# A state-space layer and a routed low-rank projection on one core: the order of two peeled steps, the place of one operand split, and the bank borders are changed

## The reference, cut to what matters

```
# layer 0: for each head a kernel k (sum of 64 damped modes), causal convolution of the masked rows
u  = x * (sample < length[seq]);  y = causal_conv(u, k[head]) + u * D[head]
x  = x + y * mask
# layer 1: a dense projection, and two of eight low-rank experts, picked per row
logits = x @ Wr.T + 5.0 * onehot(language);  gates = softmax over the top 2
x  = x + x @ W.T + 2.0 * sum_e gates[e] * (x @ A[e].T) @ B[e].T
```

## Time and profile before

| what | value |
|---|---|
| time, median of 3 runs | 715.37 us (712.67 to 715.88) |
| the profiled execution: its time | 714.37 us |
| the profiled execution: its span, first to last instruction | 712.6 us |
| busy share of the span: PE, DVE, ACT, POOL | 91%, 70%, 65%, 3% |
| mean granted clock of TensorE | 0.975 of full |

### The profile page before, as it was taken

How to read it: one execution, slowest core, us unless ns; L and a number is a source line. 1 busy time by engine, 2 the same in 40 slices (tenths; PEclk the granted TensorE clock), 3 DMA queues, 4 the chain that set the end, 5 groups by cost and what they waited for, 6 DMA issues and landing times.

```text
span 712.6 us, 12371 instructions
## 1 busy us (share of the span) xinstructions
PE 648.1 (91%) x3629; PEld 617.4 (87%) x3629; DVE 495.3 (70%) x1518; ACT 464.9 (65%) x980; POOL 19.1 (3%) x38
## 2 busy tenths in 40 slices
PE   3679778999999999999999999999999999999997
PEld 2478668899898989999898989989898989989997
DVE  8885665776776777766777768676777777676641
ACT  5875666767576767757577766757677776754431
POOL 0000000000000000000000000000000000000000
PEclk9699988999999999999999999999999999999999
DMA  6521122111223222123222221122232211222112
GB/s 184 165 60 31 37 67 68 33 54 47 66 66 66 66 66 41 46 45 66 66 66 66 66 52 47 34 66 66 66 66 66 61 29 57 52 66 38 39 29 60
DMA packets 23904, 43.40 MB, mean 61 GB/s; under 512 B 9896, under 2 KB 14544, under 8 KB 23888
## 3 DMA queue, kind: packets, MB, share of 16 engines
q1 hardware_dynamic: 18608, 26.42, 16.1%
q10 hardware_dynamic: 5280, 16.78, 9.5%
HBM read 26.35 MB, written 16.85 MB: 61 GB/s over the span
## 4 chain that ended last, share of the span: by engine, by line
DVE 34%; PE 22%; issue 21%; ACT 21%; DVEq 1%; ACTq 1%; DMA 0%; SPq 0%
PE pc L1159 13%; DVE state L885 11%; ACT swapped L479 9%; PE pmg L1220 7%; DVE xt L926 5%; ACT s_hi L501 3%; DVE u_lo L837 3%; ACT state L487 3%; ACT L668 2%; DVE t_lo L842 2%; DVE zo_lo L848 2%; DVE gate L959 1%; DVE held L918 1%; DVE k_col L857 1%; DVE c_lo L858 1%
## 5 line engine op out<-in xcount | busy, mean ns | idle before, releaser
L1220 PE MATMUL pmg<-w_hi,y_hi 128*128 128x388 f32 (+1 forms) x768 | 267.4, 348 | 3.1 <-DVE w_lo L828 3.1
L1220 PE MATMUL pmg<-w_lo,y_hi 128*128 128x388 f32 (+1 forms) x768 | 261.7, 341 | 0.0
L1220 PE MATMUL pmg<-w_hi,y_lo 128*128 128x388 f32 (+1 forms) x768 | 261.6, 341 | 0.0
L1220 PEld LDWEIGHTS pmg<-w_hi,y_hi 128*128 128x128 f32 x768 | 145.9, 190 | 4.1 <-DVE w_lo L828 3.6
L1220 PEld LDWEIGHTS pmg<-w_hi,y_lo 128*128 128x128 f32 x768 | 145.9, 190 | 0.4
L1220 PEld LDWEIGHTS pmg<-w_lo,y_hi 128*128 128x128 f32 x768 | 145.6, 190 | 0.0
L479 ACT ACTIVATE swapped<-state 64x128 f32<-64x128 f32 x192 | 59.3, 309 | 87.3 <-DVE state L885 86.0
L524 ACT ACTIVATE result<-pmg 128x388 f32<-128x388 f32 (+1 forms) x96 | 43.2, 452 | 71.8 <-PE pmg L1207 71.3
L885 DVE SCALAR_TENSOR_TENSOR state<-swapped,scan_tab,state 128x192 f32<-128x192 f32 (+1 forms) x240 | 73.8, 349 | 17.1 <-ACT swapped L479 12.7
L918 DVE COPY held<-lang_f 128x1 f32<-128x1 f32 x96 | 14.8, 154 | 78.5 <-PE pc L1159 76.3
L914 DVE TENSOR_TENSOR s_lo<-state,s_hi 128x896 fp32r<-128x896 f32 x32 | 35.0, 1092 | 35.5 <-ACT s_hi L501 35.5
(11 more groups left out here) (206 smaller groups left out, 1068.6 us busy)
## 6 DMA issues: line engine op xcount, KB each, us to landing
rows<-in_x SPq DMA_DIRECT2D x64, 256.0 KB, 5.4
out<-result ACTq DMA_DIRECT2D x62, 256.0 KB, 3.8
toe<-kpad SPq DMA_DIRECT2D x30, 128.0 KB, 5.2
rows<-in_L_cond_W SPq DMA_DIRECT2D x3, 512.0 KB, 6.5
result<-in_L_cond_W SPq DMA_DIRECT2D x3, 512.0 KB, 6.0
w_rows<-in_L_cond_W SPq DMA_DIRECT2D x2, 512.0 KB, 4.4
result<-in_L_cond_A SPq DMA_DIRECT2D x1, 512.0 KB, 5.7
b_rows<-in_L_cond_B SPq DMA_DIRECT2D x2, 256.0 KB, 6.7
```

What stands on the lines that cost most here:

```text
L1220: ins = nc.tensor.matmul(pm[:, n, 0:o1 - o0], y[s][:, c, :], w[:, c, o0:o1], start=(c == 0 and y is y_hi and w is w_hi), stop=(c == CH - 1 ...
```

## The change

- **Banks.** The 1160 columns of the weights (1024 outputs, 128 for A, 8 for the router) are cut at 384 and 768 instead of 388 and 776, so the banks are 384, 384 and 392 wide instead of 388, 388 and 384. Bank 0 then needs the weight tiles 0 to 2 only.
- **Head of a step.** In the loop and behind it `split_toe(b, m + 1)` stands first in a step on ACT and DVE; before, it stood behind `ratios` on ACT and behind `route` and `split_rows` on DVE.
- **The peeled steps** get new orders on ACT, DVE, PE and SP. The powers of the third group of heads are made straight from the table `tab` with no staged copy, and its steps are pulled forward; the output of pair 0 is stored from SP's queue instead of ACT's.
- **GpSimd.** The conversion of the lengths, the mask `valid` (eight instructions of 128x64), `bias` and the sorting of B (eight copies of 128x128) move to POOL from DVE and ACT. Names `vec` in that block are POOL's.

```diff
-BANKS = [(0, 388), (388, 776), (776, WCOLS)]
+BANKS = [(0, 384), (384, 768), (768, WCOLS)]
...
@@ SP
             load_toe(0, 2)
+            sp.wait_ge(px_full, 3)
+            load_rows(0, 4)
+            sp.wait_ge(pm_free, 6)
+            for h in range(2):
+                sp.dma_start(bass.AP(out.tensor, h * LEN, [[HEADS * LEN, SEQS], [1, LEN]]),
+                             result[0][h * SEQS:(h + 1) * SEQS, :]).then_inc(result_dma[0], 16)
+            store_kernel(0, 3)
+            load_toe(0, 3)
...
@@ POOL
+            pool.wait_ge(small_in, 48)
+            pool.wait_ge(consts, 4)
+            vec.tensor_copy(len_f[:, :], len_i[:, :]).then_inc(masks, 1)
+            vec.tensor_copy(lang_f[:, :], lang_i[:, :]).then_inc(masks, 1)
+            pool.wait_ge(masks, 2)
+            for c in range(CH):
+                ins = vec.tensor_scalar(valid[:, c, :], len_f[:, :], sample_no[:, c:c + 1], 0.0, ALU.subtract, ALU.max)
+            ins.then_inc(masks, 1)
+            vec.tensor_scalar(bias[:, :], expert_no[:, :], lang_f[:, :], LANG_BIAS, ALU.is_equal, ALU.mult
+                              ).then_inc(masks, 1)
+            pool.wait_ge(b_in, 32)
+            for o in range(8):
+                vec.tensor_copy(b_sorted[:, o, :, :], b_rows[:, :, o, :]).then_inc(b_ready, 1)
...
@@ ACT, peeled
             turn_first_powers(1)
+            copy_states(0, 0, first=True)
             weight(1)
-            copy_states(0, 0, first=True)
...
-            sort_b()
+            turns_of(1, False, range(2, 4))
...
+            waves(1)
             split_y(0, 0)
             weight(4)
+            weight(5)
+            split_toe(0, 1, toe_rows_back)
             copy_states(0, 1)
-            weight(5)
+            weight(6)
             swap_odd(0, 1, 0)
-            turns_of(1, False)
-            weight(6)
+            magnitudes(1, False, reused=True)
...
+            turns_of(2, False)
+            split_rows(0, 2)
+            split_y(0, 1)
+            split_ctr(0, 2)
+            split_obs(0, 2)
             evacuate(0, 0, 0)
             evacuate(0, 0, 1)
-            split_y(0, 1)
-            split_rows(0, 2)
-            split_ctr(0, 2)
-            split_obs(0, 2)
...
@@ ACT, in the loop and behind it; DVE's has the same line at its head, and loses the one behind split_rows
             def step(b, m, rows_left=True, kernels=True):
+                split_toe(b, m + 1)
                 if rows_left:
                     split_ctr(b, m + 2)
...
                 ratios(b, m)
-                split_toe(b, m + 1)
...
@@ DVE, peeled
             rotate_first_powers(1)
-            low_weight(1)
-            split_ctr(0, 1, kernel=False)
             dve.wait_ge(chunk_ready, 1)
             scanning = scan_states(0, 0, staged=False)
             next(scanning)
+            split_ctr(0, 1, kernel=False)
+            low_weight(1)
...
             low_weight(10)
+            rotate_powers(1, False)
             split_gated(0, 0)
             merge(0, 1)
-            rotate_powers(1, False)
+            angles(2)
+            split_rows(0, 2)
             split_y(0, 1)
-            split_rows(0, 2)
             split_ctr(0, 2)
...
@@ PE, peeled
             turn_weight(4)
-            control(0, 1)
             pe.wait_ge(merged, 1)
             turn_weight(5)
+            control(0, 1)
...
-            pe.wait_ge(wlo_ready, w_tile(3) + 1)
+            pe.wait_ge(wlo_ready, w_tile(2) + 1)
             project(0, 0, 1, 0, 4)
...
             pe.wait_ge(wlo_ready, WTILES)
+            turn_rows(0, 2)
             project(0, 0, 2, 0, 4)
-            turn_rows(0, 2)
+            pe.wait_ge(gthi_ready, 1)
+            pe.wait_ge(gtlo_ready, 1)
+            turn_powers(0, 2)
...
-            turn_powers(0, 2)
             control(0, 2)
...
-            project(0, 1, 0, 0, 4)
+            project(0, 1, 0)
             turn_rows(0, 3)
-            project(0, 1, 0, 4, 8)
             project(0, 1, 1)
+            project(0, 1, 2, 0, 4)
             turn_gates(0, 1, 4)
             convolve(0, 2)
             add_loras(0, 1)
             control(0, 3)
-            project(0, 1, 2, 0, 7)
+            project(0, 1, 2, 4, 8)
```

More of the change, by code:

```diff
@@ L340, in step @@
                 load_toe(b, m + 3)
-            with sp.Fori(0, LOOPS) as b:
+            step(0, 1)
+            with sp.Fori(1, LOOPS) as b:
                 for m in range(2):
@@ L369, in stage_scan @@
                                 ).then_inc(scan_staged, 1)
-            with pool.Fori(0, LOOPS) as b:
+            pool.wait_ge(scan, SCAN * 2)
+            stage_scan(1)
+            with pool.Fori(1, LOOPS) as b:
                 pool.wait_ge(z2_ready, b + 2)
@@ L592, in _ @@
             swap_odd(0, 1, 2)
-            waves(1)
             weight(8)
-            split_toe(0, 1, toe_rows_back)
             split_states(0, 1)
             weight(9)
-            magnitudes(1, False, reused=True)
+            swap_powers(1)
             ratios(0, 0)
             weight(10)
+            turn_powers(1, False)
             split_gated(0, 0)
-            swap_powers(1)
-            turn_powers(1, False)
+            turns_of(2, False)
[3 more added lines that the diff above has]
+            split_obs(0, 2)
             evacuate(0, 0, 0)
             evacuate(0, 0, 1)
-            split_y(0, 1)
-            split_rows(0, 2)
-            split_ctr(0, 2)
-            split_obs(0, 2)
[L610 to L615, removed]
+            magnitudes(2, False, reused=True)
             split_obs(0, 3)
             evacuate(0, 0, 2)
-            split_rows(0, 3)
[L619 to L624, removed]
+            copy_states(0, 2)
+            split_ctr(0, 3)
+            waves(2)
+            swap_odd(0, 2, 0)
+            swap_odd(0, 2, 1)
+            nc.scalar.activation(warm[:, :], phase[:, 0:1], ACT.Exp)
+            swap_odd(0, 2, 2)
+            split_states(0, 2)
+            split_toe(0, 2)
+            swap_powers(2)
+            ratios(0, 1)
+            split_rows(0, 3)
             split_gated(0, 1)
-            waves(2)
+            turn_powers(2, False)
             evacuate(0, 1, 0)
@@ L630, in _ @@
             copy_states(0, 3)
[L631 to L636, removed]
+            for n in range(3):
+                swap_odd(0, 3, n)
             split_states(0, 3)
             def step(b, m, rows_left=True, kernels=True):
+                split_toe(b, m + 1)
                 if rows_left:
@@ L1019, in _ @@
             low_weight(4)
+            low_weight(5)
+            split_toe(0, 1, toe_rows_back)
             scanning = scan_states(0, 1, staged=False)
             next(scanning)
-            low_weight(5)
+            low_weight(6)
             next(scanning)
-            low_weight(6)
-            angles(1)
+            powers(1)
             next(scanning)
@@ L1043, in _ @@
             dve.wait_ge(scan_staged, 1)
-            for _ in scan_states(0, 2):
-                pass
+            scanning = scan_states(0, 2)
+            next(scanning)
+            split_obs(0, 3)
+            split_ctr(0, 3)
+            next(scanning)
+            powers(2)
+            next(scanning)
+            next(scanning)
             split_states(0, 2)
-            split_ctr(0, 3)
-            split_obs(0, 3)
+            split_toe(0, 2)
             route(0, 1)
             split_rows(0, 3)
-            split_toe(0, 2)
-            angles(2)
             split_gated(0, 1)
+            rotate_powers(2, False)
             merge(0, 2)
-            powers(2)
             split_y(0, 2)
@@ L1102, in turn_weight @@
                                   B_: (b_ready, b_sorted)}[what]
-                pe.wait_ge(loaded, 1 if what == B_ else 16)
+                pe.wait_ge(loaded, 8 if what == B_ else 16)
                 before = [j for j in range(k) if TILE[j][1] is place]
@@ L1278, in _ @@
             turn_weight(7)
+            project(0, 0, 0, 6, 8)
             pe.wait_ge(v_copied, 2)
```

36 lines of the change are left out of this document (10 added, 26 removed).

## The result

The changed kernel takes 671.31 us (median of 4 runs, 671.07 to 673.04); the kernel before takes 714.71 in the same call (712.67 to 715.88). The ratio is 0.9401, with a 95% interval of 0.9373 to 0.9429. The profiled execution took 673.04 us, with a span of 671.2 us at a granted clock of 0.983; the one before had 714.37, 712.6 and 0.975. Profiled against profiled, 41.3 us are gone. The changed kernel's own runs, here and in e5, lie at two values, about 673.1 at a clock of 0.983 and about 671.1 at 0.989 to 0.993.

A forecast was written before the change was run, and what follows sets the result against it. PE was taken to bound the kernel, with 23 us of t_lo waits in the loop and 17 us idle in the peeled steps. 714.4 - 24.1 - 19.7 = 670.6, so 671 us; forecast 665 to 675 (chance 0.62), ends 664 and 688.

The forecast's parts named there:

- The split at the head: In the loop, t_lo is held by DVE's order alone; moving it to the step's head saves 24.1 us.
- Shorter step: Loop step occurring 14 times: the gap of 0.74 us before the convolution shrinks, saving 0.7 us each (0.6 to 0.71).
- Longer step: Second step of each loop iteration, 13 times: saves 1.1 us each (0.95 to 1.2), a 0.3 us wait for gated staying.
- the wait moves rather than goes: Loop: t_lo ahead of route makes gated late in both kinds of step; 12 us saved, 683 us; chance 0.08.
- Bank borders: Bank widths cost nothing in the loop; in the peel, bank 0 loses its 2.25 us wait for W's fourth block.
- The peeled steps: First convolution to pair 3's: new orders bring pair 3's convolution to 100.5 from 120.2 us, 19.7 us saved.
- the floor and its waits: Peeled steps: full-clock work 62.1 us plus half clock and waits gives 69.7, from 31.9; pair 3's convolution at 101.6.
- placement: Peeled steps: operations placed with their traced durations, without queue latencies, put pair 3's convolution at 99.4 us.
- The rival with only half of the peel's gain: Peeled steps: a missed wait holds PE, most likely w_lo tiles between scan rounds; 10 us gained, 680 us; chance 0.17.
- The rival of a late sort: GpSimd sorts B late, delaying turn_weight(9); slower from 94 us on, 718 us if ending at 98; chance 0.03.
- DVE pays nothing: Head of the kernel: POOL waits for DVE and DVE's own times stay unchanged, so nothing was taken on DVE.
- The rival that hung on it: Head: DVE and POOL hold each other up, so scans of pairs 0 and 1 come later; +4 us, 675; chance 0.08.

The follow-up runs named there:

- e5: The changed kernel run again without any edit; 673.12 us, ratio 0.9414 to the kernel before.
- e1: The kernel before with one edit, the Toeplitz split at the head of a step in the loop and behind it; 692.98 us, ratio 0.97.
- e2: The changed kernel with the Toeplitz split put back behind route and ratios in the loop; 696.75 us, ratio 0.9744 to the kernel before.
- e3: The changed kernel with bank borders back at 388 and 776 and the wait for the fourth block of W; 673.83 us.
- e8: The changed kernel with the loop's powers behind route on DVE and ACT's Exp table load behind copy_states; 664.36 us, ratio 0.9306 to the kernel before.
- e7: The changed kernel with ACT's Exp table load in the loop moved earlier, right behind copy_states; 666.45 us, ratio 0.9337 to the kernel before.
- e9: The changed kernel with DVE's t_lo between route and u_lo, ACT's half of the split staying at the head; 670.05 us.
- e6: The changed kernel with the powers of the next chunk behind route in DVE's loop; 666.27 us, ratio 0.9322 to the kernel before.
- e11: The changed kernel with powers behind route and the Exp table load earlier, in the loop and also in the peeled steps; 664.8 us.
- e4: The changed kernel with GpSimd's work back: masks on DVE, B sorted by one ACT instruction between two swaps; 674.87 us.
- e10: The changed kernel with only the sorting of B back on ACT, the masks staying on GpSimd; 675.99 us.

## Why the prediction was right, step by step

**The sum.** Forecast from the profiled execution: 24.1 off in the loop, 19.7 in the peel, 43.8 in all. Measured between the two spans: behind the convolution of pair 3, 712.6 - 120.23 = 592.4 became 671.2 - 101.84 = 569.4, 23.0 less; ahead of it 18.4 less. That is 41.4, and 41.3 in the time. The forecast of 671 met the median of 671.31, but not for every reason. The profiled executions would have said 670.6 and measured 673.04, and 1.3 of the difference is in the peel, 1.1 in the loop.

**The split at the head.** Right in mechanism and nearly in size. e1 alone gives 23.0, and in e2 the waits come back. Shorter step: 19.83 to 19.13 is 0.70, forecast 0.7. Longer step: 20.71 to 19.70 is 1.01, forecast 1.1 with bounds of 0.95 to 1.2. The forecast for two steps was 38.8 and 38.83 was measured. The term that was too big is the longer step's. I had `gated` and the transpose moved by 0.34 us and the convolution 0.14 us behind the transpose. A wait of 0.18 us is left (forecast 0.3), and the convolution starts 0.24 us behind it: those 0.1 us, 13 times, are the 1.1 us by which 24.1 was too much. The rival "the wait moves rather than goes" is out: it needed 39.6 us for two steps.

**Bank borders.** Costed at nothing in the loop, and at nothing they came (e3: 19.68 and 19.12). Their use in the peel, the wait at 51.85 of the earlier trace rows, is there: 2.51 us come back without them.

**The peeled steps.** Two estimates stood side by side, and I took 100.5 between 101.6 (the floor and its waits) and 99.4 (placement). Measured was 101.84. The sum of floor and waits seems right, but its terms missed and cancelled:

| term of the peeled steps, us | forecast | changed kernel |
|---|---|---|
| PE's waits | 5.9 | 4.5 |
| lost at half clock | 1.7 | 4.5 (estimate) |
| PE's work at full clock | 62.1 | 61.0 (estimate) |
| from the first convolution to pair 3's | 69.7 | 69.96 |

The second row is worked out from the stretches shown above: 2 x (0.12 x 24.10 + 0.08 x 20.34) = 9.0 us at the half level, and half of it lost; the third is what is left. So the term that was mis-sized is the clock, by 2.8 us. Of the single waits, 0.5, 0.3 and 0.4 were forecast and 0.44, 0.35 and 0.39 measured; 2.1 for `gated` at pair 2 measured 2.00; 1.5 at pair 3 measured 0.92. The 1.1 for `merge` is not listed in the changed kernel (0.41 in e5, 0.73 in e8), and 0.29 for pair 3's state at 90.81 was not forecast. The first convolution was forecast at 31.9 and came at 31.88; nine executions of the same code up to there lie between 31.69 and 32.16, so the last digits are luck. The rival with only half of the peel's gain would have put pair 3 near 110; it is out.

**What I missed there is the clock.** I wrote that it would be at full from some 37 us on. In the profiled execution it was 0.92 from 81.5 to 101.84, and 0.50 from 82 to 84 us: behind the wait of 2.00 us, the matmuls of pair 2's convolution ran at the half level of 1.2 GHz. This is the tile's summary for the convolution of pair 2 in the changed kernel (times in ns: min, median, max):

```profile
L1171 PE MATMUL pc<-u_hi,t_lo x2: 572/600/628, 81.9 to 83.2; 128*128 128x512 f32 x2
```

The same instructions in e8, in which this part of the program is the same:

```profile
L1171 PE MATMUL pc<-u_hi,t_lo x2: 393/396/398, 82.1 to 82.8; 128*128 128x512 f32 x2
```

In e7, e8 and e9 the step from pair 2 to pair 3 takes 18.87 to 19.02 us, in the changed kernel, e5 and e6 20.44 to 20.47, with the same peeled code and the same wait (1.95 to 2.01 us). So the fall of the clock costs 1.5 us, and it comes or not by the execution; what decides it is open. Without it pair 3's convolution comes at 99.79, 100.44 and 100.39: the forecast of 100.5 is met where the clock stays up, as I had assumed, and missed by the clock's 1.5 us where it falls. It can be part of the 2 us between a run of 671.1 at 0.99 and one of 673.1 at 0.983; as no run of the changed kernel at 0.99 was traced, that is argued. The wait was shortened in e11 alone, to 1.09 us, with another coming in its place. The clock stayed up there, but so it did in e8 with 2.00 us; that a kernel without the wait would keep its clock is not shown.

**GpSimd.** It takes 19 instructions off the others, and not 18: two conversions, eight masks, `bias` and eight copies. POOL's count rises by 18 (38 to 56), as one copy of `gen_tab` is gone. Forecast: masks done by 31 us, the sort by 53. GpSimd in order of time:

```profile
14.09 4.64 POOL L375 TENSOR_SCALAR valid<-len_f,sample_no 128x64 int32<-128x64 f32 x8
...
19.45 2.27 POOL L381 COPY b_sorted<-b_rows 128x128 f32<-128x128 f32 x8
```

All of it is done at 21.7. A copy of 128x128 takes 326 ns at the median and not the 1.6 us that the elements of the 196 ns copy gave: so most of those 196 ns is fixed, which was my other bound. The rival of a late sort is far off; it needed 94 us.

"DVE pays nothing" was wrong in sign and harmless in size. Beside GpSimd's work, from 13 to 22.5 us, DVE in the changed kernel (mean ns of one behind the comma):

```profile
L828 DVE TENSOR_SCALAR far_turn<-tab 128x64 f32<-128x64 f32 x2 | 0.3, 240 | 0.0
L822 DVE TENSOR_TENSOR scratch<-scratch 64x64 f32<-64x64 f32 x1 | 0.2, 247 | 0.0
```

and in the kernel before, in the same stretch:

```profile
L810 DVE TENSOR_SCALAR far_turn<-tab 128x64 f32<-128x64 f32 x2 | 0.3, 186 | 0.0
L791 DVE TENSOR_TENSOR scratch<-scratch 64x64 f32<-64x64 f32 x1 | 0.2, 208 | 0.0
```

Some small DVE instructions are 39 to 54 ns longer: of seventeen of the 64x64 kind in this stretch four take 246 to 249 ns, and most of the rest stay near 208. The long ones are not longer (w_lo 1225 and 1224 ns); they also read one of their tensors from TensorE's output, so that it is their length is not shown. The u_lo behind them starts at 16.31 in the place of 16.11: 0.2 us. e4, with the masks back on DVE, has 184 ns again for the first kind and 207 to 209 for the second, one of 218 apart. So it is GpSimd's work that lengthens them. The Trainium skill (GPSIMD Engine Reference, Specifications) says that GpSimd shares its SBUF interfaces with VectorE and that the two contend where a VectorE instruction has two SBUF inputs; by the `scratch` rows, which are of that kind, the trace agrees, and now on DVE's side. The `far_turn` rows read one tensor and are longer too. The rival that hung on it had 4 us, and 0.2 came. Against it stands the 0.7 us (0.5 to 1.1) that e4 and e10 show as the gain of the move.

## What to carry to other kernels

An instruction whose operand has long been there, but which stands in an in-order queue behind one that is late, is worth looking for: here one move of 0.34 us of DVE work, from behind u_lo to ahead of it, gave 23 us. When the first wait is gone, compare the long and the short kind of step again: the 0.57 us still between them was two further moves on other engines, and they didn't add. For a head or tail that is reordered by hand, sum the floor of the bounding engine, its half-clock time and each wait that is left, and afterwards compare term by term: here the total came out within 0.3 us while the half-clock term was 2.8 us too small. And before a start that is 0.8 us later is put down to an edit, look at how far it moves between executions of the same code, here 0.5 us.

## What the runs showed of the hardware

- Behind a wait of PE of 1.95 to 2.01 us, in a stretch otherwise at full clock, the clock fell to the half level for some 3 us in five executions (changed, e4, e5, e6, e10), at a cost of 1.5 us, and stayed at full in five others (e2, e3, e7, e8, e9).
- The issue of a store on ACT's queue took 3.88 and 4.00 us in the place of 0.5 to 0.6 in two kernels, with the DMA engines at 3 and 4 GB/s meanwhile; what holds it is open. It is not the time at which ACT gets there (e3: 100.51, 0.59 us).
- GpSimd's strided fp32 copy of 128x128 takes 326 ns at the median, beside 196 for 128x16 when DVE does not hold it up.
- Small DVE instructions (64x64, 128x64) beside GpSimd's masks and sort take up to 54 ns longer in part; those of 1.2 us do not.
- Two steps take 38.83 us with banks of 384, 384 and 392 columns, and 38.80 with 388, 388 and 384.
